# Sixty-four bytes in front of the work buffers of a two-layer graph attention kernel

## The reference

```python
# layer 0 ("A" in the kernel)
q, k, v = x @ Wq.T + bq, x @ Wk.T + bk, x @ Wv.T + bv        # split into 8 heads
pros = softmax(where(adj == 0, -16384, einsum('bhnd,bhmd->bhnm', q, k)))
z = v
for _ in range(4):
    z = 0.9 * einsum('bhnm,bhmd->bhnd', pros, z) + 0.1 * v
x = layernorm(x + z) * gamma + beta
# layer 1 ("B")
nx = layernorm(x) * ln1_g + ln1_b
q, k, v = nx @ wq + bq, nx @ wk + bk, nx @ wv + bv
bias = where(adj > 0, 0.1 * adj * adj, -inf)
attn = softmax(einsum('bhqd,bhkd->bhqk', q, k) / sqrt(32) + bias)
x1 = x + (attn @ v) @ wo + bo
n2 = layernorm(x1) * ln2_g + ln2_b
out = x1 + gelu(n2 @ w1 + b1) @ w2 + b2                        # 256 -> 1024 -> 256
```

## Time and profile before

| | |
|---|---|
| median of 3 runs | 2363.1 us (2363.02 to 2365.95) |
| the profiled execution | 2364.01 us |
| its span, first to last instruction | 2362.2 us |
| PE busy | 2282.8 us, 97% |
| ACT busy | 1919.9 us, 81% |
| DVE busy | 1745.2 us, 74% |
| POOL busy | 1510.8 us, 64% |
| DMA, mean of 16 engines | about 11% of the span |

### The profile page before, as it was taken

The page is one execution under the profiler, slowest core; times in us unless marked ns, Lnnn a source line. Parts: engine busy times, 40 slices in busy tenths (PEclk is TensorE's granted clock), DMA queues, the critical chain, the costliest instruction groups (busy, mean ns, idle before and its releaser), DMA issues.

```text
span 2362.2 us, 77819 instructions
## 1 busy us (share of the span) xinstructions
PE 2282.8 (97%) x29492; PEld 2175.0 (92%) x29492; DVE 1745.2 (74%) x7009; ACT 1919.9 (81%) x6462; POOL 1510.8 (64%) x1610
## 2 busy tenths in 40 slices
PE   2799999999999999999999999999999999999987
PEld 2689999999999999999999999999999999999987
DVE  2578778777777777777777877877877877877863
ACT  0678888888888888888888888888888888888874
POOL 0676666666666666666666666666666666666652
PEclk9999999999999999999999999999999999999999
DMA  3110110110110111011011011011011011011000
GB/s 96 35 33 24 33 38 25 33 38 25 33 38 26 31 38 31 27 38 31 27 38 37 20 37 38 20 38 37 20 37 38 20 37 38 22 35 38 20 15 15
DMA packets 95729, 76.85 MB, mean 33 GB/s; under 512 B 9600, under 2 KB 95104, under 8 KB 95360
## 3 DMA queue, kind: packets, MB, share of 16 engines
q1 hardware_dynamic: 95360, 71.87, 9.9%
HBM read 55.06 MB, written 16.78 MB: 30 GB/s over the span
## 4 chain that ended last, share of the span: by engine, by line
PE 93%; ACT 3%; DVE 1%; issue 1%; POOL 0%; DMA 0%; ACTq 0%; DVEq 0%; POOLq 0%
PE ring_ps L288 41%; PE ring_ps L405 15%; PE ring_ps L351 13%; PE ring_ps L343 10%; PE score_ps L334 6%; PE ring_ps L371 5%; PE ring_ps L298 3%; ACT probs L439 1%; ACT hidden L467 0%; ACT hT_high L467 0%; DVE w_low L504 0%; POOL probs L681 0%; DVE probs L539 0%; ACT zT L453 0%; ACT L467 0%
## 5 line engine op out<-in xcount | busy, mean ns | idle before, releaser
L439 ACT ACTIVATE probs<-probs,negmax 128x128 f32<-128x128 f32 x2048 | 796.4, 396 | 11.6 <-DVE negmax L539 4.5
L681 POOL TENSOR_TENSOR probs<-probs,rinv 128x512 f32<-128x512 f32 x512 | 533.0, 1062 | 113.3 <-DVE rinv L553 113.3
L439 ACT ACTIVATION_READ_ACCUMULATOR probs<-probs,negmax 128x1 f32 x2048 | 399.8, 195 | 0.0
L453 ACT ACTIVATE zT<-ring_ps 128x512 f32<-128x512 f32 x256 | 158.1, 618 | 213.4 <-PE ring_ps L351 213.4
L288 PE MATMUL ring_ps<-inT_C_high,w_high 128*128 128x256 f32 x1024 | 305.5, 298 | 1.5 <-DVE inT_C_low L520 1.4
L343 PE MATMUL ring_ps<-ident,probs 128*128 128x128 f32 x2048 | 295.0, 277 | 6.2 <-POOL probs L681 4.4
L405 PE MATMUL ring_ps<-w_high,hT_high 128*128 128x256 f32 x1024 | 299.1, 292 | 1.8 <-ACT hT_high L467 1.5
L288 PE MATMUL ring_ps<-inT_C_high,w_low 128*128 128x256 f32 x1024 | 289.6, 283 | 0.0
L288 PE MATMUL ring_ps<-inT_C_low,w_high 128*128 128x256 f32 x1024 | 289.4, 283 | 0.0
L405 PE MATMUL ring_ps<-w_high,hT_low 128*128 128x256 f32 x1024 | 288.1, 281 | 0.0
L405 PE MATMUL ring_ps<-w_low,hT_high 128*128 128x256 f32 x1024 | 287.1, 280 | 0.0
(11 more groups left out here) (148 smaller groups left out, 7377.1 us busy)
## 6 DMA issues: line engine op xcount, KB each, us to landing
xT_sb<-in_xT_dram SPq DMA_DIRECT2D x64, 256.0 KB, 3.1
x_sb<-in_x_dram SPq DMA_DIRECT2D x64, 256.0 KB, 2.8
out_dram<-x SPq DMA_DIRECT2D x128, 128.0 KB, 2.0
adj_A<-in_adj_dram SPq DMA_DIRECT2D x64, 128.0 KB, 3.1
adj_B<-in_adj_dram SPq DMA_DIRECT2D x64, 128.0 KB, 2.3
probsT_A<-in_L_gnn_w_dram SPq DMA_DIRECT2D x1, 1024.0 KB, 7.5
probsT_B<-in_L_gnn_w_dram SPq DMA_DIRECT2D x1, 1024.0 KB, 9.2
probs<-in_L_gnn_Wq_dram SPq DMA_DIRECT2D x1, 256.0 KB, 2.9
```

Of the source, the lines that this page charges most:

```text
L439: e = act.activation(probs[:, u, h, :], probs[:, u, h, :], ACT.Exp, bias=negmax[:, u, h:h + 1], scale=-1.0, accum_out=sums[:, u, h:h + 1])
L453: act.activation(zT[k][:, :, :, :], ring(name, g).rearrange("p (b c n) -> p b c n", b=GB, c=C), ACT.Copy).then_inc(s_out[name], 1)
L681: pool.tensor_tensor(probs[:, u, hs, :], probs[:, u, hs, :], rinv[:, u, hs].unsqueeze(2).to_broadcast([P, HR, P]), ALU.mult).then_inc(s_pr ...
```

## The change

A buffer of 16 float32 per partition, 64 bytes, is allocated between the constants and the work buffers. Nothing reads or writes it.

```diff
         tenth, eps, minus_half = sb("tenth", [P, 1]), sb("eps", [P, 1]), sb("minus_half", [P, 1])
 
+
+
+        sb("apart", [P, 16])
         x_sb = sb("x_sb", [P, GB, H])
         xT_sb = sb("xT_sb", [P, C, T])
```

## The result

The changed kernel takes 2345.87 us (median of 6 runs, 2343.09 to 2348.55) against 2364.22 us for the kernel before on the same chips (6 runs, 2363.02 to 2365.95). The ratio is 0.9922, with a 95% interval of 0.991 to 0.9934. It is faster by 18 us, or 0.8%. 2314 us was forecast, a gain of 49 us: the direction and the place were right, the size was 2.7 times too large.

The account below looks back on a forecast made before the run. PE was taken as the bound, busy 97% of the span. From 2364.0 us, 49 came off for dense products (other terms 0), giving 2315.0, and 2314 with the median 0.9 lower; range 2266 to 2382 us.

Parts of the forecast that it names:

- the chain's beat: Mid-run, the same piece returns every 35.22 us; each nanosecond off PE's spacing shortens the round, over 64 rounds.
- Taking POOL at no cost: POOL's work buffers moving off 0 modulo 128 cost nothing: 1283 ns with a row at 32, 1286 at 0.
- The wobble of the products: Behind a transpose, dense products start 0.11 then 0.12 us apart with no wait, read as a collision inside PE.
- In between I take half of the excess, 57 us: Dense products: 11520 times about 0.010 us above the transposes' spacing is 115 us; half of it was taken as gain.
- different pace: Products stream 256 columns while 128 load, so the distance does not stay and some meetings remain; reason for half.
- The allowance for ACT: Where ACT is late PE will wait, so a seventh comes off the gain: 57 x 0.86 = 49 us.
- The distance does nothing: Rival on dense products: excess belongs to the fp32r load, or reads meet equally often; 2363 us, chance 0.26.
- The transposes start to collide: Rival at transposes going from 32 to 96 apart: up to 36 us lost, 2399 us; slower in all 0.24.
- products that pay more: Slower side at dense products: 0.4 ns more each is 4.7 us; within the 0.24 for slower.
- The rival that all excess goes: Dense products fall to the transposes' 0.109 us, 1.8 us less per round: around 2264 us, chance 0.13.

Follow-up runs that it names:

- 128-byte kernel: Full kernel with the unused buffer at 128 bytes in place of 64: 2372.15 us, ratio 1.0027 to the kernel before.
- the first experiment: TensorE-only program, dense products at 13 operand distances, 12 transposes at each shift: last steps 113.3 ns at 192 ahead, 120.0 at 0; transposes 109.1 throughout.
- the two full kernels with equal distances and different places: Changed kernel's buffer at 192 bytes; or 64 unused bytes below the weights and 192 behind the constants: 2341.07 and 2341.38 us, ratios 0.989 and 0.9889.
- 32-byte kernel: Full kernel with the unused buffer at 32 bytes in place of 64: 2368.78 us, ratio 1.0012 to the kernel before; run again, 2368.34 us.

## Why the prediction was right in direction and wrong in size

**The bound was read rightly.** PE had no gap in a round before and has none after, ACT kept 5 us; the gain is that of the spacing, round by round, as the chain's beat had promised.

**The place of the effect was read rightly.** Dense products changed, transposes and head products did not, and ACT's and DVE's busy times in a round changed by 1% at most. Taking POOL at no cost from the earlier trace rows was not exact: its product of `y` and `gamma_row` took 1737 ns before, 1795 after and 1634 in the 128-byte kernel. POOL is far from the bound, so this had no weight here. The wobble of the products in the earlier trace rows with nothing waited for was the sign of it. The experiment with TensorE alone shows that it lies in that engine and depends on addresses; the two full kernels with equal distances and different places show that it is the distance that counts among starts that are multiples of 64.

**The term that failed is "In between I take half of the excess, 57 us".** The excess went from 118.66 - 109 = 9.7 ns per product to 7.5, so less than a quarter of it went: 0.34 us in each of 64 rounds are 21.8 us, 18.7 us in the span, where 57 and then 49 were forecast. The half was a midpoint between bounds with a reason, different pace, for staying below all; no row supported the value itself. The count was too high as well: 11520 takes in all 180 products of a round, and only 158 steps shrank. Two things behind the half were wrong. The distance was taken modulo 128, so all stages seemed to go from 0 to 64 and to gain alike. It counts modulo 256 and with its sign, so the stages split into 192 ahead (96 products, of which 60 reached 113.9) and 64 ahead (84 products, 117.8). And 109, the spacing of transposes that move 128 columns, was taken as within reach of products that move 256, while the lowest steady spacing found at 256 moving columns, in 64 distances and 8 starts, is 113.3.

**The allowance for ACT was not needed.** PE's waits for other engines came to about 76 us before and 77 after, none of them between 600 and 1000 us, where PE was busy throughout in both traces, and the round lost all of the 0.34 us that the spacings give.

**The rivals.** "The distance does nothing" falls with the first experiment. "The transposes start to collide" falls at all 13 shifts. A slower outcome was possible by the products, as its text allows (products that pay more): with 128 unused bytes the kernel took 0.27% more than the kernel before. The rival that all excess goes is excluded by the 113.3. The argument of different pace, that some meetings remain from any start, agrees with the floor but was not itself tested.

**What stays open** is how the two reads meet. Distance, start modulo 32 and the number of loaded columns set a few patterns. Why one piece settles at 117.8 and the next at 113.3 from equal addresses is not shown; it repeats with the place of the piece in the round.

## What to carry to other kernels

Where PE is the bound and its products follow each other with no wait, compare their start-to-start spacing between groups of one shape: a spread of a few per cent can come from the addresses of the operands alone. Then set the distance of moving and stationary operand on purpose, for each product by its role, and measure two or three distances; for fp32r products of 128 x 128 by 256 here, with starts at multiples of 64, 192 bytes ahead modulo 256 was best. To have it in all of them took the weights in another order and two unused buffers, of 128 and 192 bytes, and turned 2368 us into 2332. With 64 loaded columns 192 was not the best distance, so another shape wants a measurement of its own. And before such a kernel is compared with another, check that an added or dropped small buffer has not shifted everything behind it: 128 unused bytes made this one slower, 192 made it faster.

## What the hardware showed that was not expected

- Spacing of dense products from 113.3 to 126.7 ns at equal shape and clock, by the operands' start addresses alone, in repeating patterns (113 113 114; 118 117 118; 119 121; 115 117 122 120 119).
- The spacings of the pieces whose steps are all alike differ by whole multiples of 3.3 ns, which is 8 periods of 2.4 GHz: 113.3, 116.7, 120.0 and 126.7 with 256 moving columns, 173.3 and 180.0 with 384, 226.7 with 512.
- Two or more such patterns at the same addresses, kept to the end of the piece once entered.
- A settled pattern is reached only after up to 13 products, so a piece of 12 can end before it.
- Float32 transposes at 109.1 ns at every shift tried.
- One execution of the 32-byte kernel took 12475.5 us, with dense products most often 0.64 us apart, a recorded clock of 1.00 and ACT's busy time nearly as ever (1999.0 us); the other nine lay between 2366.87 and 2368.99 us. Its cause is not known.
